# Cross-attention on one core: k and z transposed by the DMA instead of TensorE, and first scores behind two query tiles

## The chip, the cores and the metric

The kernel runs on one core of a Trainium2 chip. The metric is the device time of one execution in microseconds (us), the time of the slowest core, here the only one.

## The reference

Eight batches of `x` and `ctx`, 256 rows of 1024 features each; 32 heads of 32 features.

```python
mu, var = mean(x), var(x)
z = (x - mu) * rsqrt(var + LN_EPS) * ln_gamma + ln_beta
Q = split_heads(z @ Wq.T); K = split_heads(ctx); V = split_heads(ctx)
scores = einsum('bhsd,bhtd->bhst', Q, K) * 32 ** -0.5
scores = where(mask, scores, -inf)
attn = einsum('bhst,bhtd->bhsd', softmax(scores), V)
out = x + attn @ Wout.T
```

## The kernel before, in words

**Numbers.** Every float32 operand of a product is kept as two float16 values, hi and lo (the rest after hi), and a product is three float16 passes (hi·hi, hi·lo, lo·hi). For the scores the three passes lie on top of each other in the contraction: `q_stack` holds for each head 32 rows of hi, 32 of lo, 32 of hi, then a row of ones; `k_stack` holds hi, hi, lo, then the mask row and three constant rows that carry the log-sum-exp in the second pass. So one matmul contracts over 97 rows (first pass) or 100 (second).

**Stages.** A prologue transposes Wq and Wout (TensorE writes the transpose of a 128x128 block to PSUM, ScalarE takes hi, VectorE lo), normalises and transposes x of batch 0, and makes its q. Then come eight iterations, one for each batch b. In **phase S**, 16 steps n = 0..15 (four heads and 128 query rows each), TensorE makes scores (`scores_s`, L499), VectorE their maximum (L826), ScalarE exponentials with row sums (L653). In **phase T**, eight groups g with two steps each, TensorE makes the scores transposed and already normalised (`scores_t`, L525), ScalarE takes the exponential (L670), TensorE multiplies by v (`probs_times_v`, L537) and the result is split into `aT` (L676, L861). Between these steps TensorE does output-projection matmuls of batch b-1 (L478, 7 in each S step, `O_AT`) and q matmuls of batch b+1 (L453, in the last two S steps and in T). Score tiles are double buffered, so step n waits for step n-2.

**The operands of the next batch.** In S steps 0 to 3 TensorE also transposes z of batch b+1 (`z_transposes`, L415, from `x_nat` that VectorE has normalised at L817), and in steps 6 to 9 k (`k_transposes`, L428). VectorE scales them out of PSUM into `t_f32` (L769 with gamma and beta, L777), GpSimd (POOL) splits them into hi and lo (L326 to L338). Then SP, whose queue is strictly in the order of the program, issues twelve copies and a mask copy for each half of `k_stack` (`fill_k_stack`, L168, L172), twelve for each half of `q_stack` (`fill_q_stack`, L189), and the rows of the log-sum-exp (`fill_l_rows`, L203), for which the first `scores_t` of each half waits. `add_residual` (L868) on VectorE stands in S steps 6, 8, 11 and 14; the seventh output matmul of step 6 begins a new PSUM tile and waits for the one of step 6.

**Order.** Everything is written out by hand: each engine has its own program and waits on semaphores. The first scores of batch 0 stand behind all four q tiles and half of Wout; the other eight Wout blocks (`WO_STEPS`) lie in iteration 0.

## Time and profile before

| | |
|---|---|
| median of 3 runs | 629.6 us (628.39 to 630.53) |
| the profiled execution: its own time | 630.62 us |
| its span | 628.8 us |
| mean granted TensorE clock | 0.975 |
| prologue, to the first scores | 60 us |
| iteration 0 | 68 us |
| iterations 1 to 6 | 70.3 us each |
| iteration 7 with the last projection | 77.8 us |

The span runs from the first to the last instruction of the profiled execution; its own time is 1.8 us more. The iterations are read off by the first scores of each batch, which repeat every 70.3 us. Busy time says how long an engine had an instruction in it, idle time with its releaser says what it waited for; the chain of work that ended last gives, piece by piece, what set the pace.

### The profile page before, as it was taken

The numbers are of one execution on the slowest core, as the hardware profiler recorded it, in microseconds if no ns is written. First come the engines' busy times: TensorE is split into PE (matmuls) and PEld (weight loads), VectorE is DVE, ScalarE is ACT, GpSimd is POOL, SyncE is SP. The second block draws the span as 40 slices with busy tenths as digits, with TensorE's granted clock in tenths as the row PEclk, the third lists the DMA queues.
The fourth block names the chain that finished last, engine by engine and source line by source line (L and its number), as shares of the span: only waits on it lengthen the run. The fifth ranks groups of instructions, "written<-read, shape, count | busy, mean of one in ns | idle before, by whom it ended". The sixth has DMA issues, their size and how long they took to land.

```text
span 628.8 us, 12852 instructions
## 1 busy us (share of the span) xinstructions
PE 589.5 (94%) x4769; PEld 396.2 (63%) x4769; DVE 385.0 (61%) x841; ACT 430.8 (69%) x1321; POOL 112.8 (18%) x131
## 2 busy tenths in 40 slices
PE   4878879999999999999999999999999999998897
PEld 4667657655776567655776567755776567644443
DVE  5575977478654885388654886288645882278211
ACT  3342978778766886678766886678666885699740
POOL 2320440035000530044000520044001520000000
PEclk9889689999999999999999999999999999999899
DMA  9774321443344252343344152333344132321202
GB/s 282 267 223 128 114 73 55 122 126 99 106 117 130 60 163 56 107 117 105 100 125 130 52 170 57 99 119 109 96 124 134 63 89 57 98 51 67 71 1 101
DMA packets 37344, 68.62 MB, mean 109 GB/s; under 512 B 9009, under 2 KB 11041, under 8 KB 37282
## 3 DMA queue, kind: packets, MB, share of 16 engines
q1 hardware_dynamic: 36994, 67.60, 35.9%
q8 instruction: 38, 0.62, 0.4%
q10 hardware_dynamic: 288, 0.20, 0.1%
q14 instruction: 24, 0.20, 0.1%
HBM read 33.56 MB, written 8.39 MB: 67 GB/s over the span
## 4 chain that ended last, share of the span: by engine, by line
PE 71%; DVE 14%; ACT 8%; issue 3%; DMA 2%; ACTq 1%; SPq 1%; DVEq 0%
PE mm L453 24%; PE mm L478 17%; PE pv L537 10%; PE score L525 9%; PE score L499 6%; DVE nmax L826 6%; ACT score L653 6%; PE pv L415 2%; PE pv L428 2%; DMA ctx_sb<-in_ctx 1%; ACT probs L670 1%; DVE o_buf L868 1%; PE pv L382 1%; DVE wqT L748 1%; DVE t_f L777 1%
## 5 line engine op out<-in xcount | busy, mean ns | idle before, releaser
L653 ACT ACTIVATE score<-score,nmax 128x256 f32<-128x256 f32 x512 | 230.1, 465 | 47.7 <-DVE nmax L826 47.6
L453 PE MATMUL mm<-zT,wqT 128*128 128x256 f16 x1536 | 186.6, 276 | 0.0
L826 DVE TENSOR_REDUCE nmax<-score 128x2 f32<-128x512 f32 x256 | 163.8, 684 | 37.0 <-PE score L499 36.9
L478 PE MATMUL mm<-woT,aT 128*128 128x512 f16 x768 | 183.6, 379 | 1.5 <-DVE o_buf L868 1.5
L670 ACT ACTIVATE probs<-score 128x1024 f32<-128x1024 f32 x128 | 123.9, 1022 | 73.4 <-PE score L525 73.1
L453 PEld LDWEIGHTS mm<-zT,wqT 128*128 128x128 f16 x1536 | 151.5, 99 | 23.0 <-issue 2.9
L478 PEld LDWEIGHTS mm<-woT,aT 128*128 128x128 f16 x768 | 74.7, 97 | 73.2 <-DVE o_buf L868 4.4
L653 ACT ACTIVATION_READ_ACCUMULATOR score<-score,nmax 128x1 f32 x512 | 114.7, 224 | 0.0
L861 DVE TENSOR_TENSOR aT<-pv,aT 128x256 f16<-128x256 f32 x64 | 26.9, 423 | 114.7 <-ACT aT L676 113.9
L499 PE MATMUL score<-k_stack,q_stack 97*128 97x256 f16 x512 | 79.6, 279 | 10.5 <-ACT score L653 9.4
L499 PEld LDWEIGHTS score<-k_stack,q_stack 97*128 97x128 f16 x512 | 47.9, 99 | 46.4 <-ACT score L653 22.9
L326 POOL CAST zT<-t_f 128x512 f16<-128x512 f32 x28 | 17.1, 609 | 322.0 <-DVE t_f L769 322.0
L525 PE MATMUL score<-q_stack,k_stack 100*128 100x256 f16 x512 | 68.3, 276 | 2.0 <-ACT probs L670 1.1
L537 PE MATMUL pv<-probs,ctx_sb 128*32 128x256 f32 x1024 | 69.4, 389 | 0.9 <-DVE aT L861 0.6
L525 PEld LDWEIGHTS score<-q_stack,k_stack 100*128 100x128 f16 x512 | 45.7, 98 | 29.2 <-issue 18.1
L537 PEld LDWEIGHTS pv<-probs,ctx_sb 128*32 128x32 f32 x1024 | 27.5, 110 | 25.9 <-ACT probs L670 8.0
L645 ACT ACTIVATE qT<-mm 128x512 f16<-128x512 f32 x32 | 19.5, 608 | 23.0 <-PE mm L453 23.0
L782 DVE SCALAR_TENSOR_TENSOR qT<-mm,qT 128x512 f16<-128x512 f32 x32 | 22.0, 689 | 20.5 <-ACT qT L645 20.0
L328 POOL TENSOR_TENSOR zT<-t_f,zT 128x512 f16<-128x512 f32 x28 | 32.3, 1155 | 2.2
L338 POOL TENSOR_TENSOR kT<-t_f,kT 128x512 f16<-128x512 f32 x28 | 32.3, 1155 | 2.2
L868 DVE SCALAR_TENSOR_TENSOR o_buf<-mm,res 128x512 f32<-128x512 f32 x32 | 21.7, 679 | 17.3 <-PE mm L478 17.3
L676 ACT ACTIVATE aT<-pv 128x256 f16<-128x256 f32 x64 | 24.8, 390 | 9.0 <-PE pv L537 9.0
(62 smaller groups left out, 352.2 us busy)
## 6 DMA issues: line engine op xcount, KB each, us to landing
k_stack<-kT SPq DMA_DIRECT2D x192, 64.0 KB, 2.0
q_stack<-qT SPq DMA_DIRECT2D x180, 64.0 KB, 2.0
x_nat<-in_x SPq DMA_DIRECT2D x8, 1024.0 KB, 5.4
ctx_sb<-in_ctx SPq DMA_DIRECT2D x8, 1024.0 KB, 6.3
res<-in_x SPq DMA_DIRECT2D x32, 256.0 KB, 2.9
out<-o_buf SPq DMA_DIRECT2D x32, 256.0 KB, 2.0
probs<-in_L_xattn_Wq SPq DMA_DIRECT2D x8, 512.0 KB, 7.8
probs<-in_L_xattn_Wout SPq DMA_DIRECT2D x8, 512.0 KB, 4.5
```

The lines of the kernel that those rows point to most:

```text
L328: pool.tensor_tensor(zT[:, 1, at], t_f32[:, f % 2], zT[:, 0, at], ALU.subtract).then_inc(split_done, 1)
L338: pool.tensor_tensor(kT[:, 1, at], t_f32[:, f % 2], kT[:, 0, at], ALU.subtract).then_inc(split_done, 1)
L453: last = pe.matmul(mm[i % 2][:, m2 * S:(m2 + 1) * S], wqT[:, wp, k, m * P:(m + 1) * P], zT[:, zp, k, :], start=(v2 == 0), stop=(v2 == KT * ...
L478: last = pe.matmul(mm[i % 2][:], aT[:, ap, k, st * P:(st + 1) * P], woT[:, wp, k, nh * 512:(nh + 1) * 512], start=(v == 0), stop=(v == O_M ...
L499: last = pe.matmul(score[n % 2][:, j, :], q_stack[0:S_ROWS, h, j, gl, st * P:(st + 1) * P], k_stack[0:S_ROWS, pb, h, j, gl, :], start=True ...
L525: last = pe.matmul(score[n % 2][:, j, :], k_stack[0:T_ROWS, pb, h, j, gl, tt * P:(tt + 1) * P], q_stack[0:T_ROWS, h, j, gl, :], start=True ...
L537: last = pe.matmul(pv[g % 2][DH * j:DH * (j + 1), 0, :], ctx_sb[:, pb, tt, g * P + DH * j:g * P + DH * (j + 1)], probs[:, g % 2, tt, j, :] ...
L653: last = act.activation(score[n % 2][:, j, :], score[n % 2][:, j, :], ACT.Exp, bias=nmax[:, st, h, j, gl:gl + 1], accum_out=sums[:, st, h, ...
L670: act.activation(probs[:, g % 2, tt], score[n % 2][:], ACT.Exp).then_inc(exp_done, 1)
L826: dve.tensor_reduce(nmax[:, st, h, at, gl], score[n % 2][:, at, :], AX.X, ALU.max, negate=True).then_inc(max_done, 1)
L861: dve.tensor_tensor(aT[:, 1, g, :], pv[g % 2][:, 0, :], aT[:, 0, g, :], ALU.subtract).then_inc(a_lo, 1)
L868: dve.scalar_tensor_tensor(out=o_buf[:, i % 2, :], in0=mm[i % 2][:], scalar=1.0 / W_SCALE, in1=res[:, i % 2, :], op0=ALU.mult, op1=ALU.add ...
```

## The change

k and z are no longer transposed by TensorE. z is normalised with gamma and beta in its natural layout by VectorE in two passes (`centre`, `normalise`), k stays as it came. GpSimd splits both in natural layout: for k it writes, for 16 heads and 128 rows at a time (one of four pieces c), 32 columns of hi, 32 of hi, 32 of lo and 32 extra ones (mask, constants) side by side. Then SP issues DMA transposes: four for z (256 KB each) and four for k (512 KB each) of a batch. k's transposed block is the stack itself, so its 24 row copies and two mask copies fall away. The natural pieces lie in `probs`, which is free in phase S (for batch 1 in `aT`, `res`, `o_buf`; for batch 0 in the other half of `k_stack`). GpSimd's pieces 2 and 3 of k wait until pieces 0 and 1 have been transposed; ScalarE's first exponentials of phase T wait for the transposes to be done with `probs`. In the prologue the first scores stand behind two q tiles; the other two, the last two Wq blocks, centring of batch 1 and all sixteen Wout blocks lie in iteration 0. The kernel's factors of 0.5 on k and 2 on q are gone.

```diff
+            def turn_z(a):
+                for st in range(ST):
+                    sp.wait_ge(z_lo, (a - 1) * ST + st + 1)
+                    if a == 1 and st == 0:
+                        sp.wait_ge(q_ready, FILLS)
+                    for part in range(2):
+                        sp.dma_start_transpose(zT[:, part, :, st * P:(st + 1) * P], z_nat(a)[:, st, part]).then_inc(z_in, DMA)
+
+            def turn_k(a, pa, c):
+                sp.wait_ge(k_done, 2 * (4 * a + c + 1))
+                if a == 1 and c == 0:
+                    for h in range(2):
+                        sp.wait_ge(k_in[h], 2 * DMA)
+                sp.dma_start_transpose(k_turned(pa, c), k_nat(a, c).rearrange("p n d -> p (n d)")).then_inc(k_in[c // 2], DMA)
...
-                if not first and not last:
-                    sp.wait_ge(pv_ready, b * G)
-                    load_c(b + 1, 1 - pb)
                 if not first:
+                    if not last:
+                        sp.wait_ge(pv_ready, b * G)
+                        load_c(b + 1, 1 - pb)
                     sp.wait_ge(q_lo, b * FILLS + 4)
                     fill_q_stack(1)
+                    if not last:
+                        turn_z(b + 1)
                     store_out(b - 1, 0)
                     load_res(b - 1, 2)
+                    if more:
+                        load_x(b + 2)
+                    if not last:
+                        turn_k(b + 1, 1 - pb, 0)
+                        turn_k(b + 1, 1 - pb, 1)
                     store_out(b - 1, 1)
                     load_res(b - 1, 3)
-                if not last:
-                    fill_k_stack(b + 1, 1 - pb, 0)
-                if more:
-                    sp.wait_ge(fill_ready, z_fill(b + 1, 3) + 1)
-                    load_x(b + 2)
-                if not first:
+                    if not last:
+                        turn_k(b + 1, 1 - pb, 2)
+                        turn_k(b + 1, 1 - pb, 3)
                     store_out(b - 1, 2)
                 fill_l_rows(b, 0)
                 fill_l_rows(b, 1)
...
-                             rows[0:1, r, :].unsqueeze(1).to_broadcast([1, 2 * H, S])).then_inc(row_in, DMA)
-            sp.wait_ge(mask_ok, 1)
-            sp.dma_start(mask_add, mask_st).then_inc(mask_in, DMA)
-            for n in range(4, KT):
-                load_w(n)
+            sp.wait_ge(ones_done, 2)
+            sp.dma_start(q_stack[96:97].rearrange("o h j g s -> o (h j g) s"), one_f16.unsqueeze(1).to_broadcast([1, H, S])).then_inc(row_in, DMA)
+            load_w(4)
+            load_w(5)
+            turn_k(0, 0, 0)
             sp.wait_ge(z0_ready, FILLS)
...
+            turn_k(0, 0, 1)
+            load_w(6)
+            turn_k(0, 0, 2)
+            load_w(7)
+            turn_k(0, 0, 3)
             load_c(1, 1)
...
+            sp.wait_ge(q_hi, 1)
+            for j in range(J):
+                sp.dma_start(q_stack[0:DH, 0, j, 0:2], qT[DH * j:DH * (j + 1), 0, 0:2, :]).then_inc(q0_in, DMA)
             load_w(KT)
+            fill_q0_tile_1()
             load_w(KT + 1)
-            fill_q0_tile(0, (0, 1))
...
-            fill_q0_tile(1, range(J))
-            fill_k_stack(0, 0, 1)
+            sp.wait_ge(q_lo, FILLS)
+            fill_q_stack(1)
             load_w(KT + 4)
             load_w(KT + 5)
-            sp.wait_ge(q_lo, FILLS)
-            fill_q_stack(1)
+            turn_z(1)
+            load_x(2)
             load_w(KT + 6)
             load_w(KT + 7)
+            for c in range(4):
+                turn_k(1, 1, c)
...
+            def z_split(a, st):
+                pool.wait_ge(norm_done, a * ST + st + 1)
+                if a > 1 and st == 0:
+                    pool.wait_ge(pv_ready, (a - 1) * G)
+                pool.tensor_copy(z_nat(a)[:, st, 0], x_nat[:, st]).then_inc(z_hi, 1)
+                pool.wait_ge(z_hi, (a - 1) * ST + st + 1)
+                pool.tensor_tensor(z_nat(a)[:, st, 1], x_nat[:, st], z_nat(a)[:, st, 0], ALU.subtract).then_inc(z_lo, 1)
...
+                pool.tensor_copy(to[:, :, 0:2 * DH].rearrange("p n (r d) -> p n r d", r=2), of.unsqueeze(2).to_broadcast([P, HEADS, 2, DH])).then_inc(k_hi, 1)
+                pool.tensor_copy(to[:, :, 3 * DH:3 * DH + K_EXTRA], k_extra[:, a, tt].unsqueeze(1).to_broadcast([P, HEADS, K_EXTRA])).then_inc(k_done, 1)
+                pool.wait_ge(k_hi, 4 * a + c + 1)
+                pool.tensor_tensor(to[:, :, 2 * DH:3 * DH], of, to[:, :, 0:DH], ALU.subtract).then_inc(k_done, 1)
+
+            for c in range(4):
+                k_split(0, 0, c)
+
+            pool.wait_ge(q_hi, 1)
+            for j in range(J):
+                pool.dma_start(q_stack[2 * DH:3 * DH, 0, j, 0:2], qT[DH * j:DH * (j + 1), 0, 0:2, :]).then_inc(q0_pool_in, DMA)
...
+                pe.wait_ge(ones_done, 2)
+                pe.wait_ge(gb_in, 2 * DMA)
+                for i, bank in enumerate((mm[0], mm[1], pv[0], pv[1])):
+                    row = (gamma_row, beta_row)[i // 2][:, i % 2 * 512:(i % 2 + 1) * 512]
+                    to = bank[:] if i < 2 else bank[:].rearrange("p c s -> p (c s)")
+                    pe.matmul(to, one_f32, row, start=True, stop=True).then_inc(gb_ready, 1)
...
                     elif u == 0:
-                        pe.wait_ge(split_done, z_fill(a, 3) + 1)
+                        pe.wait_ge(z_in, a * 2 * ST * DMA)
...
                 else:
-                    pe.wait_ge(wq_lo, W_FILLS - 2 + 2 * n)
+                    pe.wait_ge(wq_lo, 8 + 2 * n)
...
-            Q_AT_STEP_FIRST = [0] * 6 + [9 * n for n in range(11)]
-            Q_AT_FIRST = [104 + 11 * g for g in range(G)] + [187, Q_ALL]
+
+            Q0_AT = [2 * Q_MM + 24 * n for n in range(5)]
+            Q_AT_STEP_FIRST = [0] * 12 + [0, 16, 32, 48, 64]
+            Q_AT_FIRST = [96 + 12 * g for g in range(G)] + [186, Q_ALL]
...
-                    if not last:
-                        if n in Z_STEPS:
-                            z_transposes(b + 1, Z_STEPS.index(n), b)
-                        if n in K_STEPS:
-                            k_transposes(b + 1, 1 - pb, K_STEPS.index(n), b)
+                    if first and n < 4:
+                        q_matmuls(0, Q0_AT[n], Q0_AT[n + 1], None)
+                    if first and n == 0:
...
             for i in range(FILLS):
                 z0_transposes(i)
             for f in range(4, 8):
                 wq_transposes(f)
             q_matmuls(0, 0, Q_MM, None)
-            for f in range(8, 12):
+            for f in range(8, 10):
                 wq_transposes(f)
-            for i in (2, 3):
-                k0_transposes(i)
             q_matmuls(0, Q_MM, 2 * Q_MM, None)
-            for f in range(12, W_FILLS):
+            for f in range(10, WQ_EARLY):
                 wq_transposes(f)
-            for f in range(WO_FIRST // 2):
-                wo_transposes(f)
-            q_matmuls(0, 2 * Q_MM, 3 * Q_MM, None)
-            for f in range(WO_FIRST // 2, WO_FIRST):
-                wo_transposes(f)
-            q_matmuls(0, 3 * Q_MM, 4 * Q_MM, None)
-            pe.wait_ge(row_in, (1 + L_ROWS) * DMA)
             iteration(0, 0, True, False)
...
+                if first and n == 0:
+                    act.wait_ge(wo_ready, W_FILLS)
+                elif n == 0 and not last:
+                    act.wait_ge(k_in[1], 2 * (b + 2) * DMA)
+                elif n == 2 and not first and not last:
+                    act.wait_ge(z_in, (b + 1) * 2 * ST * DMA)
                 act.activation(probs[:, g % 2, tt], score[n % 2][:], ACT.Exp).then_inc(exp_done, 1)
...
+
+            def centre(a, st):
+                dve.wait_ge(rstd_step, (a + 1) * RSTD_STEPS)
+                if known(a, 0):
+                    dve.wait_ge(gb_done, 4)
+                dve.scalar_tensor_tensor(out=x_nat[:, st], in0=x_nat[:, st], scalar=mean_var[:, st, 0:1], in1=gamma_b[:],
+                                         op0=ALU.subtract, op1=ALU.mult).then_inc(centre_done, 1)
+
             def normalise(a, st):
-                dve.wait_ge(rstd_step, (a + 1) * RSTD_STEPS)
-                dve.tensor_scalar(x_nat[:, st], x_nat[:, st], mean_var[:, st, 0:1], rstd[:, st:st + 1],
-                                  ALU.subtract, ALU.mult).then_inc(norm_done, 1)
+                dve.wait_ge(centre_done, a * ST + st + 1)
+                dve.scalar_tensor_tensor(out=x_nat[:, st], in0=x_nat[:, st], scalar=rstd[:, st:st + 1], in1=beta_b[:],
+                                         op0=ALU.mult, op1=ALU.add).then_inc(norm_done, 1)
...
                 for n in range(STEPS):
                     max_step(b, n)
-                    if not last:
-                        if n - 1 in Z_STEPS:
-                            z_scale(b + 1, Z_STEPS.index(n - 1))
-                        if n - 1 in K_STEPS:
-                            k_scale(b + 1, K_STEPS.index(n - 1))
+                    if first and 1 <= n < 5:
+                        if n == 1:
+                            for f in range(WQ_EARLY, W_FILLS):
+                                wq_split(f)
+                        if n < 3:
+                            centre(1, n - 1)
+                        else:
+                            normalise(1, n - 3)
+                    if first and n in (2, 4):
+                        q_split(0, 1 + n // 2)
                     if first and n - 1 in WO_STEPS:
-                        wo_split(WO_FIRST + WO_STEPS.index(n - 1))
-                    if first and n == Q_STEP_FIRST:
-                        q_split(b + 1, 0)
+                        for f in WO_STEPS[n - 1]:
+                            wo_split(f)
```

TensorE, phase S of batch 1, steps 0 to 3 and 6 of before (`x_nat` is x of the next batch, `ctx_sb` its k):

```order
L499 MATMUL score<-k_stack,q_stack 128x256 x4
L415 MATMUL pv<-ident,x_nat 128x128 x4
L478 MATMUL mm<-woT,aT 128x512 x7
L499 MATMUL score<-k_stack,q_stack 128x256 x4
L415 MATMUL pv<-ident,x_nat 128x128 x4
L478 MATMUL mm<-woT,aT 128x512 x7
...
L499 MATMUL score<-k_stack,q_stack 128x256 x4
L428 MATMUL pv<-ident,ctx_sb 128x128 x4
L478 MATMUL mm<-woT,aT 128x512 x7
```

The same steps of the change:

```order
L501 MATMUL score<-k_stack,q_stack 128x256 x4
L478 MATMUL mm<-woT,aT 128x512 x7
L501 MATMUL score<-k_stack,q_stack 128x256 x4
L478 MATMUL mm<-woT,aT 128x512 x7
L501 MATMUL score<-k_stack,q_stack 128x256 x4
```

Eight groups of four transposes have left the row; scores and output matmuls follow each other directly.

SP, from the last `q_stack` copies of a batch to the log-sum-exp rows, before:

```order
L189 DMA q_stack<-qT 32x1024 x12
L214 DMA out<-o_buf 128x512
L209 DMA res<-in_x 128x512
L214 DMA out<-o_buf 128x512
L209 DMA res<-in_x 128x512
L168 DMA k_stack<-kT 32x1024 x12
L172 DMA k_stack<-k_stack 1x16x256
L152 DMA x_nat<-in_x 128x2x1024
L214 DMA out<-o_buf 128x512
L203 DMA q_stack<-l_rows 1x16x256 x6
```

and of the change:

```order
L208 DMA q_stack<-qT 32x1024 x12
L195 DMA_TRANSPOSE zT<-probs 128x8x128 x4
L235 DMA out<-o_buf 128x512
L230 DMA res<-in_x 128x512
L174 DMA x_nat<-in_x 128x2x1024
L202 DMA_TRANSPOSE k_stack<-probs 128x16x128 x2
L235 DMA out<-o_buf 128x512
L230 DMA res<-in_x 128x512
L202 DMA_TRANSPOSE k_stack<-probs 128x16x128 x2
L235 DMA out<-o_buf 128x512
L221 DMA q_stack<-l_rows 1x16x256 x6
```

All eight transposes now stand ahead of the log-sum-exp rows in SP's queue; before, one half of the k copies did, the other came behind them.

TensorE, from the first q tile to step 4 of the first batch, in the change (before, 4 blocks of 48 L453 and eight Wout blocks stood ahead of the first scores):

```order
L453 MATMUL mm<-zT,wqT 128x256 x48
L402 MATMUL score<-ident,probs 128x128 x8
L453 MATMUL mm<-zT,wqT 128x256 x48
L402 MATMUL pv<-ident,probs 128x128 x16
L501 MATMUL score<-k_stack,q_stack 128x256 x4
L453 MATMUL mm<-zT,wqT 128x256 x24
L402 MATMUL pv<-ident,probs 128x128 x8
L501 MATMUL score<-k_stack,q_stack 128x256 x4
L453 MATMUL mm<-zT,wqT 128x256 x24
```

Two q tiles are cut into four pieces of 24 matmuls and stand behind scores 0 to 3.

## Rows read from the trace of the kernel before

**Rows 1.** The page, busy time and share of the span of each engine.

```profile
PE 589.5 (94%) x4769; PEld 396.2 (63%) x4769; DVE 385.0 (61%) x841; ACT 430.8 (69%) x1321; POOL 112.8 (18%) x131
```

**Rows 2.** Busy time by stretch: length, engines, granted clock, DMA share, GB/s.

```profile
61.00:129.00 68.00, 60.35 (x516) 44.44 (x514) 48.37 (x106) 54.32 (x168) 14.11 (x16) 0.87 0.31 87
340.10:410.40 70.30, 69.17 (x582) 46.77 (x580) 45.75 (x102) 51.25 (x160) 14.12 (x16) 1.00 0.36 107
551.00:628.80 77.80, 69.08 (x446) 32.70 (x444) 33.05 (x66) 47.56 (x156) 0.00 (x0) 0.97 0.18 59
```

**Rows 3.** The chain of waits in iteration 4: start us, us, what.

```profile
346.98 0.44 PE pv L415 x4
347.42 1.51 PE mm L478 x7
348.94 0.44 PE score L499 x4
...
353.92 0.68 DVE nmax L826
354.61 0.61 DVE o_buf L868
355.26 0.39 PE mm L478
...
364.58 0.60 DVE t_f L777
...
374.04 5.02 PE mm L453 x46
```

**Rows 4.** Groups by line: xcount, busy us, mean ns of one, idle before.

```profile
L415 PE MATMUL pv<-ident,x_nat 128*128 128x128 f32 x112 | 18.2, 287 | 0.2
L861 DVE TENSOR_TENSOR aT<-pv,aT 128x256 f16<-128x256 f32 x64 | 26.9, 423 | 114.7 <-ACT aT L676 113.9
L855 DVE TENSOR_TENSOR l_rest<-l_rest,l_rows 16x256 f32<-16x256 f32 x16 | 6.6, 413 | 0.6
L336 POOL CAST kT<-t_f 128x512 f16<-128x512 f32 x28 | 17.1, 610 | 42.5 <-DVE t_f L777 42.5
L338 POOL TENSOR_TENSOR kT<-t_f,kT 128x512 f16<-128x512 f32 x28 | 32.3, 1155 | 2.2
```

**Rows 5.** Timeline of SP's queue in iteration 4: start us, us issuing, what.

```profile
339.65 8.01 SPq L189 DMA_DIRECT2D q_stack<-qT  x12
372.53 13.14 SPq L203 DMA_DIRECT2D q_stack<-l_rows  x6
```

**Rows 6.** DMA issues: xcount, KB each, median us from issue to landing.

```profile
probs<-in_L_xattn_Wq SPq DMA_DIRECT2D x8, 512.0 KB, 7.8
q_stack<-l_rows SPq DMA_DIRECT2D x48, 8.0 KB, 1.8
```

**Rows 7.** Busy time by stretch, the ten us in which the DMA moved most.

```profile
30.00:40.00 10.00, 8.90 (x80) 7.87 (x78) 5.77 (x10) 6.43 (x13) 3.48 (x4) 1.00 1.02 295
```

**Rows 8.** Timeline of VectorE and TensorE in the prologue: start us, us, what.

```profile
11.87 1.54 DVE L817 TENSOR_SCALAR x_nat<-x_nat,mean_var,rstd 128x1024 f32<-128x1024 f32 x2
...
21.80 6.40 PE L453 MATMUL mm<-zT,wqT 128*128 128x256 f16 x48
...
59.98 0.60 PE L499 MATMUL score<-k_stack,q_stack 97*128 97x256 f16 x4
```

**Rows 9.** The chain of waits in iteration 0: Wq and Wout splits, exponentials.

```profile
34.20 2.48 DVE wqT L748 x4
...
99.53 0.49 ACT woT L638
100.02 1.82 ACT score L653 x8
...
103.19 1.84 ACT probs L670 x2
...
128.33 0.55 PE score L499 x4
```

445 lines of the change are left out of this document (194 added, 251 removed).

## The prediction

> **What bounds the kernel now.** I read the page first: TensorE is busy 94% of the span, ScalarE 69%, VectorE 61%, GpSimd 18% [rows 1]. A share is an average, so next came the busy time by stretch: iterations 1 to 6 are alike, 70.3 us long with 69.2 us of TensorE, iteration 0 takes 68.0 us at a granted clock of 0.87, and the last stretch is the loosest [rows 2]. The chain of waits then says what a TensorE instruction is worth. In phase S it runs along TensorE: four transposes 0.44 us, seven output matmuls 1.51, four scores 0.44 [rows 3]. A step with transposes lasts 2.39 us, one without 1.95. Phase T is TensorE alone, and nothing is removed there. So what leaves TensorE in phase S is worth its time, down to the next limit. That limit is near: ScalarE needs 1.82 us for a step's eight instructions [rows 9], against 1.95 on TensorE.
>
> **Iterations 1 to 6, what is removed.** Eight steps lose 0.44 us each, 3.5 us. One is no gain: in step 6 the seventh output matmul waits for VectorE's maximum and residual, until 355.26 [rows 3]; without transposes TensorE arrives 0.44 us earlier and waits 0.44 longer, since VectorE starts only once the scores are there. Near the end of phase S the chain is VectorE's, and k's last scaling stands in it with 0.60 us [rows 3]; it goes, but TensorE's own pace of 1.95 a step comes next, so I count 0.4. Together 7 x 0.44 + 0.4 = 3.5 us an iteration, 6 x 3.5 = **21 us**. The bounds are 2.6 (ScalarE's waits eat two steps) and 3.9 (step 6 gains too). Iteration 7 has nothing to lose.
>
> **What is added there, on VectorE.** Two normalising instructions of 0.8 us (1.54 for a pair [rows 8]) become four with two SBUF inputs. The nearest row is L855, 413 ns for 256 elements [rows 4], about 0.15 us plus an element a ns; so some 1.2 us for 1024, and 4.8 - 1.5 = 3.3 us more. They stand in phase T, groups 3 to 6, where VectorE sat idle for 114.7 us over 64 splits, 14 us a batch [rows 4]. Cost zero; without that cover 20 us in six iterations.
>
> **On GpSimd.** Per batch: z twice 1024 elements cast and subtracted, 2 x (2 x 0.61 + 2 x 1.16) = 7.1 us by the 512-element rows L336 and L338 [rows 4]; k four pieces of 1024 cast, 512 copied, 512 subtracted, 1.2 + 0.6 + 1.2 = 3.0 us each. That is 19 us in 67, hidden, but its order matters: z is ready 3.5 and 7 us into phase S, k's pieces 0 and 1 at 10 and 13, pieces 2 and 3 only after the first two have been turned.
>
> **On SP: the term that decides.** Let t be the time that one k piece (512 KB) holds the queue; a z piece is half. No row shows a DMA transpose. From below: the DMA moved 295 GB/s at its fullest [rows 7], 512 KB in 1.8 us. From above: eight 64 KB copies at SP's 8.01 / 12 = 0.67 us [rows 5], 5.3 us. The queue after the start of phase S: twelve q copies until 8.3 us; z until 8.3 + 2t; the output store not before 14 (residual of step 6), some loads 1.2; k 0 and 1, 2t; landing about 2 (the 8 KB copies land in 1.8 [rows 6]); GpSimd 3.0 to 6.0; k 2 and 3; then the log-sum-exp rows, three issues of 0.6 and 1.8 to land. `scores_t` wants them when the q matmuls of 5.02 us [rows 3] are done, at 31.4 + 5.0 = 36.4 us. With t = 1.8 all is turned at 28.7 and the rows land at 32.5: no wait. With t of 3 or more SP never idles, and they land at 18.6 + 6t, which is on time up to t = 3.0. I take t = 2, near the lower end: a transpose is one issue and moves the bytes of one 512 KB load, not of eight row copies. **Cost zero.**
> The Trainium skill (Advanced Engine Details and Errata, X-Bar Transpose (TRN2)) says that such transposes run at 350 to 400 GB/s, which would make t about 1.4, an estimate; no run here shows it yet. It changes nothing in the sum. Against the change speaks the skill's VectorE: DVE Perf Modes, The three transpose paths: 1309 ns by DMA for a 128x128 block where TensorE takes 390. If these did not overlap, a k piece of 16 blocks would take 21 us and the kernel over 900; an estimate by that page, which the sum does not use.
>
> **Prologue and iteration 0.** Before: q starts at 21.8 us, first scores at 60.0, first exponentials of phase T at 103.2, next batch at 128.3 [rows 8, 9]. Now: the mask, gamma and beta stand ahead of VectorE's chain (about 2 us) and normalising takes 3.3 us more; the splits after it are the same. I put q's start at 26 to 27. Two q tiles of 6.4 and 5.4, six groups of Wq transposes, with VectorE's second statistics between, bring the first scores to **44 us**, 16 earlier. But their work moves into phase S. Steps 0 to 4 hold on VectorE five maxima (6.5 us), two Wq splits (1.2, by 2.48 for four [rows 9]), four normalising passes (4.8), two q splits (1.4), 14 us, plus waits for 24 q matmuls at a time: 17.6. Then ScalarE sets the pace: eleven steps of 1.82 + 0.49 and four more Wout splits, 27.4, plus 2 for the log-sum-exp. First exponentials at 91 instead of 103.2, **12 us** won. Phase T costs 0.7 more (12 q matmuls a group for 11) and batch 1's k pieces 2 and 3 are turned late, 1 to 2 us. Net **10 us**, from 5 to 16.
>
> **Sum.** The profiled execution took 630.6 us, 1.0 over the median of 629.6. 630.6 - 21 - 10 = 599.6, against the median **599 us**.
>
> **Rivals.**
> A, *slower queue*: t = 3.4, between the two ends. The rows land at 39.0 instead of 36.4, and seven phases T start 2.6 us late: 599 + 18 = **617 us**. For it: SP needs 0.67 us even for 64 KB. Against: a 512 KB load lands in 7.8 us at the crowded start [rows 6], with others ahead of it. Chance 0.14.
> B, *SP's queue becomes the bound* (the other sign): one mechanism, the eight transposes ahead of the log-sum-exp rows. At t = 5.3 they land at 50.4, 14 us late, seven times over: 599 + 98 = **697 us**. It turns the gain of 31 into a loss from 4.4 us of wait per batch, t = 3.8. TensorE's clock would then dip in each wait, as in iteration 0. The skill's 1309 ns lies far beyond. Chance 0.10.
> C, *VectorE and GpSimd in each other's way in the prologue*: k's four pieces run on GpSimd from about 12 to 24 us, the four normalising passes on VectorE fall into that time. No row shows a long two-input VectorE instruction beside GpSimd. If each waits for a GpSimd instruction of 1.2 us and Wq's splits shift with them, q starts 5 us later, and waits of step 0 to 4 take 5 more: **609 us**. The skill's SBUF - State Buffer, section SBUF: two separate sides, says that a VectorE operation with two SBUF inputs and a GpSimd operation exclude each other; the trace of before has no such pair to test it. Chance 0.12.
> D, *the gain is there but smaller*, ScalarE's 1.82 against 1.95 leaving less than I count: 2.6 an iteration, 604; inside my own range.
>
> **How the numbers follow.** My forecast (t up to 3, prologue as worked) has 0.64, and its own range is 590 to 608: the ends are 16 us of prologue with 3.9 an iteration, and 5 us with 2.6. C 0.12, A 0.14, B 0.10. The range of 590 to 620 takes in the forecast, C and A, and leaves out B and the tails. About 0.3% (1.9 us) is what a measurement of this kernel can tell from no change; all cases but B lie well below, so faster 0.87, same 0.02, slower 0.11.
>
> **What would show it.** Right: no transposes of L415 and L428, steps of 1.95 us in phase S, the iteration at 66.8 us; transposes in SP's timeline at about 2 us each; first scores at 44 us, batch 1 at 118. Wrong: TensorE waiting at `scores_t` for the log-sum-exp rows, ScalarE at its first exponential for k, POOL's k piece 2 late, the granted clock below 1.00 in iterations 1 to 6; or normalising passes longer than 1.2 us while GpSimd works.

## The result and the profile after

The changed kernel takes **656.7 us** (median of 4 runs, 653.9 to 661.8) against 629.7 (628.4 to 630.5) for the kernel before in the same session: ratio 1.0445, 95% interval 1.0392 to 1.0497. It is slower by 27 us; the forecast was 599, range 590 to 620. One of the four runs of experiment 2 (649.0 us) lay over 1.5% above the fastest of its kernel and is left out of the ratio there. The profiled execution took 655.7 us with a span of 653.9 at a mean granted clock of 0.945.

| us in the profiled execution | before | forecast | after |
|---|---|---|---|
| first q tile starts | 21.8 | 26 to 27 | 36.0 |
| first scores of batch 0 | 60.0 | 44 | 56.2 |
| batch 1 starts | 128.3 | 118.3 | 157.4 |
| iterations 1 to 6 together | 421.7 | 400.7 | 418.6 |
| iteration 7 and the last projection | 78.9 | 78.9 | 78.0 |

The lines of the table run from the first scores of one batch to those of the next. So read, batch 7 of the kernel before starts at 549.9 us, and its last stretch is 78.9 us long, where the table of the kernel before and the stretch 551.0 to 628.8 in [rows 2] have 77.8; an iteration is 70.28 us. The forecast lay 56.1 us below the profiled execution, and two lines hold it: 39.1 us up to batch 1, and 17.9 in iterations 1 to 6, less 0.9 at the end. The page of the kernel after, engines and DMA:

```profile
PE 578.7 (89%) x4537; PEld 380.6 (58%) x4537; DVE 387.6 (59%) x772; ACT 430.8 (66%) x1321; POOL 133.6 (20%) x134
DMA packets 123422, 79.86 MB, mean 122 GB/s; under 512 B 101762, under 2 KB 103202, under 8 KB 123364
```

TensorE lost 232 instructions and 10.8 us of busy time against [rows 1], yet its share fell from 94 to 89%: it waits more.

**A steady iteration.** In iteration 3, SP's queue from the start of batch 3's phase S (start, us issuing, what):

```profile
297.58 0.39 SPq L177 DMA_DIRECT2D ctx_sb<-in_ctx  x1
298.01 7.48 SPq L208 DMA_DIRECT2D q_stack<-qT  x12
305.53 6.21 SPq L195 DMA_TRANSPOSE zT<-probs  x4
...
312.90 0.45 SPq L174 DMA_DIRECT2D x_nat<-in_x  x1
313.72 7.87 SPq L202 DMA_TRANSPOSE k_stack<-probs  x2
...
326.95 4.67 SPq L202 DMA_TRANSPOSE k_stack<-probs  x2
331.66 0.97 SPq L235 DMA_DIRECT2D out<-o_buf  x1
332.68 1.97 SPq L221 DMA_DIRECT2D q_stack<-l_rows  x3
```

The chain of waits through the same place, in order of time:

```profile
319.56 4.36 DMA k_stack<-probs
...
323.98 1.04 POOL probs L358
...
334.06 2.84 DMA q_stack<-l_rows
...
336.95 1.05 PE score L525 x8
```

and TensorE there (idle time and its releaser in brackets):

```profile
329.69 0.61 PE L501 MATMUL score<-k_stack,q_stack 97*128 97x256 f16 x4 [2.13 <-ACT score L655]
330.13 5.19 PE L453 MATMUL mm<-zT,wqT 128*128 128x256 f16 x46
336.95 1.05 PE L525 MATMUL score<-q_stack,k_stack 100*128 100x256 f16 x8 [1.63 <-DMA q_stack<-l_rows]
```

Read from the top: the twelve q copies keep time, z's turns take 6.2 us, the first two k turns 7.9, they land 4.4 us after the issue, and only then may GpSimd write pieces 2 and 3 over the buffer. Their turns and a store follow, then the log-sum-exp rows, which land at 336.9, 39.3 us into the iteration; the q matmuls were done 37.7 into it. The busy time by stretch shows how full the DMA was meanwhile, in the first row those of pieces 0 and 1, in the second the whole iteration:

```profile
313.70:321.60 7.90, 7.90 (x46) 4.36 (x45) 6.31 (x14) 7.86 (x36) 0.00 (x0) 1.00 0.99 253
297.58:367.57 69.99, 65.54 (x550) 43.37 (x549) 44.49 (x92) 51.08 (x160) 17.23 (x16) 1.00 0.56 129
```

The DMA engines are full (0.99) while k is turned, behind 1 MB of x that was issued just before.

Iteration 3 is not typical in one thing: TensorE waits for the log-sum-exp rows in three of the six iterations only, 0.5, 1.6 and 0.5 us in iterations 2, 3 and 5. In all six it waits at step 15 for ScalarE, 2.0 to 2.8 us, and in three of them it then runs its q matmuls at a lower clock. Iteration 1, the slowest with 70.5 us, in three views: VectorE's log-sum-exp operations, TensorE's step 15, and the stretch behind it.

```profile
184.62 0.75 DVE L853 CAST l_rows<-l_rest 16x256 f16<-16x256 f32 x1
185.40 1.26 DVE L855 TENSOR_TENSOR l_rest<-l_rest,l_rows 16x256 f32<-16x256 f32 x1
186.69 1.01 DVE L857 TENSOR_SCALAR l_rows<-l_rest 16x256 f16<-16x256 f32 x1
```

```profile
190.32 0.61 PE L501 MATMUL score<-k_stack,q_stack 97*128 97x256 f16 x4 [2.82 <-ACT score L655]
190.77 6.85 PE L453 MATMUL mm<-zT,wqT 128*128 128x256 f16 x46
```

```profile
190.30:197.50 7.20, 7.18 (x51) 5.81 (x52) 2.85 (x8) 4.66 (x19) 0.00 (x0) 0.76 0.50 113
```

The three operations take 0.28, 0.41 and 0.28 us in the kernel before. Here GpSimd is at k's pieces 2 and 3 from 183.6 us on, beside them; the next maximum on VectorE, ScalarE's exponentials and step 15 come later by as much. The 46 matmuls take 6.85 us at a granted clock of 0.76 and 5.19 at full clock (iteration 3 above).

**Prologue.** VectorE's chain for the first rstd, and TensorE's first instructions, in two views:

```profile
13.20 0.23 DVE L939 TENSOR_SCALAR k_extra<-score 128x16 f16<-128x16 f32 x1 [5.75 <-PE score L387]
...
15.25 1.09 DVE L791 TENSOR_SCALAR newton<-var_eps 128x2 int32<-128x2 int32 x1
16.38 0.94 DVE L793 TENSOR_SCALAR rstd<-newton 128x2 int32<-128x2 int32 x1
17.36 0.51 DVE L797 TENSOR_TENSOR newton<-rstd 128x2 f32<-128x2 f32 x1
...
24.32 0.16 DVE L797 TENSOR_TENSOR newton<-rstd 128x2 f32<-128x2 f32 x1
```

```profile
5.97 3.75 PE L383 MATMUL mm<-res,l_rows 1*128 1x512 f32 x4 [5.97 <-DMA o_buf<-in_L_xattn_ln_beta]
9.52 3.62 PE L383 MATMUL pv<-o_buf,l_rows 1*128 1x512 f32 x4
12.93 0.23 PE L387 MATMUL score<-ident,l_rest 16*128 16x16 f32 x1
...
35.97 5.40 PE L453 MATMUL mm<-zT,wqT 128*128 128x256 f16 x48 [0.64 <-DVE wqT L747]
```

Two faults come together, and the first brings on the second. The mask's small transpose stands behind the row products of gamma and beta, 7.4 us, and VectorE stands behind the mask in its own program. So its chain falls into the time in which GpSimd splits k (13.60 to 24.27), and the same two-element instructions take up to 1.09 us instead of 0.16, and fall back the moment it stops. In iteration 0, steps 12 to 15 read like this on TensorE:

```profile
109.88 3.44 PE L453 MATMUL mm<-zT,wqT 128*128 128x256 f16 x16
113.15 0.60 PE L501 MATMUL score<-k_stack,q_stack 97*128 97x256 f16 x4
115.83 1.68 PE L416 MATMUL pv<-ident,probs 128*128 128x128 f32 x8 [2.07 <-DVE woT L755]
117.30 3.15 PE L453 MATMUL mm<-zT,wqT 128*128 128x256 f16 x16
```

A step takes 7.1 us (113.15 to 120.29), not 2.3: scores, 2.1 us of wait for the split of the last Wout tile, transposes, then the q matmuls, one after the other. The mean granted clock from 102 to 125 us is 0.72, so TensorE ran part of this at 1.2 and part at 2.4 GHz.

### The profile page after: what moved, and what is told of

It is laid out like the page before. It is cut to its first block, busy times and chain, and to the rows that moved or that the text cites. A ratio compares the mean times of both kernels' runs of the same rounds, so it can differ in the third digit from the quotient of the medians.

```text
span 653.9 us, 12077 instructions
## 1 busy us (share of the span) xinstructions
PE 578.7 (89%) x4537; PEld 380.6 (58%) x4537; DVE 387.6 (59%) x772; ACT 430.8 (66%) x1321; POOL 133.6 (20%) x134
## 2 busy tenths in 40 slices
DMA packets 123422, 79.86 MB, mean 122 GB/s; under 512 B 101762, under 2 KB 103202, under 8 KB 123364
## 4 chain that ended last, share of the span: by engine, by line
PE 62%; SPq 11%; DVE 10%; ACT 7%; DMA 5%; issue 3%; POOL 3%; ACTq 1%; DVEq 0%
PE mm L453 23%; PE mm L478 13%; PE pv L537 9%; PE score L525 9%; ACT score L655 5%; PE score L501 5%; SPq L202 3%; SPq L208 3%; DVE nmax L824 3%; DMA k_stack<-probs 2%; SPq L195 2%; DMA q_stack<-l_rows 1%; POOL probs L361 1%; PE pv L416 1%; POOL probs L358 1%
## 5 line engine op out<-in xcount | busy, mean ns | idle before, releaser
L453 PE MATMUL mm<-zT,wqT 128*128 128x256 f16 x1536 | 194.0, 284 | 0.6 <-DVE wqT L747 0.6
L478 PE MATMUL mm<-woT,aT 128*128 128x512 f16 x768 | 183.6, 379 | 4.1 <-DVE o_buf L868 4.1
L453 PEld LDWEIGHTS mm<-zT,wqT 128*128 128x128 f16 x1536 | 156.0, 102 | 27.4 <-issue 3.7
L501 PE MATMUL score<-k_stack,q_stack 97*128 97x256 f16 x512 | 81.0, 282 | 24.1 <-ACT score L655 17.8
L525 PEld LDWEIGHTS score<-q_stack,k_stack 100*128 100x128 f16 x512 | 45.4, 98 | 31.8 <-issue 18.5
L341 POOL CAST probs<-x_nat 128x1024 f16<-128x1024 f32 x12 | 12.4, 1036 | 235.5 <-PE pv L537 235.5
L358 POOL CAST probs<-ctx_sb 128x1024 f16<-128x1024 f32 x24 | 25.4, 1060 | 84.1 <-DMA k_stack<-probs 83.1
L868 DVE SCALAR_TENSOR_TENSOR o_buf<-mm,res 128x512 f32<-128x512 f32 x32 | 21.8, 680 | 17.3 <-PE mm L478 17.3
L361 POOL TENSOR_TENSOR probs<-ctx_sb,probs 128x512 f16<-128x512 f32 x24 | 28.3, 1178 | 0.0
```

The lines of the kernel that those rows point to most:

```text
L358: pool.tensor_copy(to[:, :, 0:2 * DH].rearrange("p n (r d) -> p n r d", r=2), of.unsqueeze(2).to_broadcast([P, HEADS, 2, DH])).then_inc(k_ ...
L361: pool.tensor_tensor(to[:, :, 2 * DH:3 * DH], of, to[:, :, 0:DH], ALU.subtract).then_inc(k_done, 1)
L453: last = pe.matmul(mm[i % 2][:, m2 * S:(m2 + 1) * S], wqT[:, wp, k, m * P:(m + 1) * P], zT[:, zp, k, :], start=(v2 == 0), stop=(v2 == KT * ...
L478: last = pe.matmul(mm[i % 2][:], aT[:, ap, k, st * P:(st + 1) * P], woT[:, wp, k, nh * 512:(nh + 1) * 512], start=(v == 0), stop=(v == O_M ...
L501: last = pe.matmul(score[n % 2][:, j, :], q_stack[0:S_ROWS, h, j, gl, st * P:(st + 1) * P], k_stack[0:S_ROWS, pb, h, gl, j, :], start=True ...
L525: last = pe.matmul(score[n % 2][:, j, :], k_stack[0:T_ROWS, pb, h, gl, j, tt * P:(tt + 1) * P], q_stack[0:T_ROWS, h, j, gl, :], start=True ...
```

## The experiments

Each was made from the changed kernel. Two theories stood at first. **Order:** the added work fits, but stands in the wrong place of a queue (SP's, TensorE's, or GpSimd against VectorE). **Worth:** what left phase S had not been worth 3.5 us, or the transposes are too dear whatever the order.

**1. The mask first.**

```diff
-            gb_rows()
             pe.wait_ge(ident_ok, 1)
             mask_transpose()
+            gb_rows()
```

> Edit: TensorE transposes the mask before it multiplies gamma and beta out to 128 rows, not behind it. Theory P (prologue): in the change VectorE's second statistics of batch 0 stand behind the mask (13.2 us), and that puts the rstd chain (14.9 to 25.1, 3.3 us of work) into the time in which GpSimd splits k (13.6 to 24.3). With the mask first, the chain runs at 8 to 12 us beside an idle GpSimd, in 3.3 us; gamma and beta (four products, some 7.2 us) then bound the centring, at about 14; q starts at 24 to 27 us instead of 36.0, and the kernel takes about 646 us instead of 656.7. Rival: the first scores (56.2 us) are bound by k's transposes in SP's queue or by the second rstd chain and not by q; then q starts earlier, but the kernel gains under 3 us. A third possibility, VectorE's two-input centring beside GpSimd: L810 and L815 then take 2 to 3 us each instead of 1.24, and half of the gain is lost.

Measured: 647.2 us, ratio to before 1.0241 (1.0185 to 1.0298); q starts at 26.7, first scores at 46.75, batch 1 at 147.7, which is 9.3, 9.4 and 9.7 us earlier; the median time is 9.5 us less (four runs, 641.2 to 650.1). In the profiled execution, 650.1 us, iterations 1 to 6 took 4.6 us more than in the changed kernel, two of them 72.6 and 73.2. So the prologue gives back what was expected, and that the median does so to the tenth is in part luck. The rstd chain runs from 8.9 to 11.8, in 3 us, since GpSimd still waits for its context load until 12.2. The mutual hold has moved to the four normalising passes. VectorE, then GpSimd:

```profile
14.25 3.72 DVE L810 SCALAR_TENSOR_TENSOR x_nat<-x_nat,mean_var,gamma_b 128x1024 f32<-128x1024 f32 x2 [2.41 <-ACT beta_b L622]
17.90 3.72 DVE L815 SCALAR_TENSOR_TENSOR x_nat<-x_nat,rstd,beta_b 128x1024 f32<-128x1024 f32 x2
```

```profile
14.86 2.04 POOL L358 CAST k_stack<-ctx_sb 128x1024 f16<-128x1024 f32 x1
```

1.86 us a pass, and GpSimd's cast takes 2.04 us where it takes 1.04 alone: both lose.

**2. In a step of iteration 0, q matmuls ahead of Wout's transposes.**

```diff
-                    if first and n in WO_STEPS:
-                        for f in WO_STEPS[n]:
-                            wo_transposes(f)
...
                         q_matmuls(b + 1, at[n], at[n + 1], c)
+                    if first and n in WO_STEPS:
+                        for f in WO_STEPS[n]:
+                            wo_transposes(f)
```

> Edit: in steps 12 to 15 of iteration 0 TensorE does its 16 q matmuls before the two Wout blocks, not behind them. Theory W: those four steps take 7.2 us each because they are one serial chain, scores, maximum, split of the last step's Wout block, this step's two blocks, 16 q matmuls (2.9 to 3.4 us, at half clock), next scores. With q first the matmuls run beside maximum and split, a step takes 3.5 to 4.5 us, and the kernel takes 645 us instead of 656.7. Rival: TensorE's own work at the low clock (0.5 to 0.7 granted) sets them; then a step takes 5 us or more and the gain is 8 us or less. Rival: batch 1's k, turned late through SP's queue (to 113.4 us), takes over; gain under 4 us.

Measured: 644.5 us, ratio 1.0164 (1.0115 to 1.0213), 12 us less, 8.2 of which lie before batch 1, which starts at 149.2. TensorE:

```profile
104.56 0.60 PE L501 MATMUL score<-k_stack,q_stack 97*128 97x256 f16 x4
105.00 1.91 PE L453 MATMUL mm<-zT,wqT 128*128 128x256 f16 x16
107.23 1.23 PE L416 MATMUL pv<-ident,probs 128*128 128x128 f32 x8 [0.32 <-DVE woT L755]
108.29 0.60 PE L501 MATMUL score<-k_stack,q_stack 97*128 97x256 f16 x4
...
119.51 1.89 PE L525 MATMUL score<-q_stack,k_stack 100*128 100x256 f16 x8 [3.83 <-DMA q_stack<-l_rows]
```

Steps fall from 7.1 to 3.73 us: the q matmuls now fill the time in which the tile is split. And a new wait appears behind them, 3.8 us for the log-sum-exp rows, whose place in SP's queue is behind batch 1's k turns.

**3. The x load behind the log-sum-exp rows.**

```diff
-                    if more:
-                        load_x(b + 2)
...
                 fill_l_rows(b, 0)
+                if more and not first:
+                    load_x(b + 2)
```

> Edit: the 1 MB load of x two batches ahead is issued behind the first log-sum-exp rows instead of just ahead of k's first transpose (batch 1 on). Theory Q1: SP's queue sets iterations 1 to 6, and its longest single piece, 5.8 us for the first k transpose against 2.0 for the later ones, is that transpose held back behind the load. Then it falls to 2 to 3 us, an iteration takes 67 instead of 69.8, and the kernel 639 us instead of 656.7. Rival Q2: it is held back by the z transposes and q copies ahead of it, whose descriptors are many; then it stays at 4.5 us or more, and the kernel within 5 us of 656.7.

Measured: 645.6 us, ratio 1.0227 (1.0196 to 1.0257). That is 11 us less where 18 were expected: the first pair of k turns falls from 7.9 to 9.3 us to 5.1 to 6.4, but iterations lie between 67.7 and 70.5. TensorE now waits for the log-sum-exp rows in none of the six, so the bytes of x ahead of the turns were what made them late. What is left stands in another place: at step 15 it still waits 1.6 to 2.8 us for ScalarE, and in the two iterations of 70.3 and 70.5 the clock falls behind that wait (0.76 and 0.77 over the q matmuls).

**4. A buffer of its own for k's pieces 2 and 3**, from batch 2 on, so that GpSimd need not wait for the first turns.

```diff
+        k_more = sb("k_more", [P, 2, HALF * J, P], F16)
...
+            elif c >= 2:
+                return k_more[:, c % 2]
```

> Edit: k's pieces 2 and 3 are split into a buffer of their own (8 KB a partition) from batch 2 on, so GpSimd doesn't wait for the transposes of pieces 0 and 1. Theory G: the chain of iterations 1 to 6 goes q copies, z, k 0 and 1, their landing, 5.7 us of GpSimd, k 3, log-sum-exp rows; without the wait it loses landing and GpSimd, some 6 to 8 us, which is more than the 3 us that phase S can shrink by, so an iteration takes 67 us instead of 69.8 (the last five of the six), the kernel 643, and VectorE's L857 falls from 531 to 281 ns since GpSimd is no longer at work beside it. Rival: the queue itself is full, k 2 and 3 are held up as long as k 0 was, and the gain is under 5 us.

Measured: 638.5 us, ratio 1.012 (1.009 to 1.015), 18 us less; iterations of 66.8 to 68.9. GpSimd's 14.6 us of wait is gone, and so is its work beside VectorE's log-sum-exp operations: the three of 16x256 from SBUF take 413, 281 and 280 ns, as before, instead of 628, 531 and 425. TensorE's wait at step 15 is 0.8 us in all six iterations, and the clock stays at full speed. Still, in four of the six the log-sum-exp rows come late, by 0.3 to 1.9 us, behind the turns of pieces 2 and 3. Of the 18 us, 13.0 lie in iterations 1 to 6. Another 5.1 lie before batch 1, where this edit changes nothing; the granted clock between 102 and 125 us was 0.85 here and 0.72 in the changed kernel. So the start of batch 1 can differ by some 5 us between profiled executions without a cause in the edit, and a difference of that size in it can't be put down to an edit.

**5. GpSimd held back in the prologue** until x of batch 0 is normalised.

```diff
+                    pool.wait_ge(norm_done, ST)
```

> The changed kernel with one wait more: GpSimd starts on batch 0's k pieces only when VectorE has normalised x (everything else as changed). Theory L (VectorE and GpSimd hold each other up on SBUF operands): the rstd chain, which took 10.2 us beside GpSimd's k split and 3.3 us in the kernel before, takes about 3.5 us again and the four normalising operations about 1.24 us each, so q starts at about 29 us instead of 36.0 and batch 1 at about 151 instead of 157.4: about 650 us, 6 less than the changed kernel. Rival M (it is only the late gamma/beta row products that make the prologue late): the chain still takes about 10 us with GpSimd idle and the time stays at 656. If k's turned pieces now come too late for the first scores, the gain is smaller than 6 us and TensorE's first score waits for k_stack instead of for q_stack.

Measured: VectorE and TensorE do as theory L says, in two views:

```profile
16.04 0.16 DVE L804 TENSOR_TENSOR rstd<-rstd,newton 128x2 f32<-128x2 f32 x1
...
17.82 2.48 DVE L811 SCALAR_TENSOR_TENSOR x_nat<-x_nat,mean_var,gamma_b 128x1024 f32<-128x1024 f32 x2
```

```profile
28.68 5.40 PE L454 MATMUL mm<-zT,wqT 128*128 128x256 f16 x48 [1.28 <-DVE wqT L748]
```

The chain takes 3.0 us instead of 10.2, the passes 1.24 each, q starts 7.3 us earlier, and rival M falls. But first scores come 3.6 and batch 1 only 5.0 us earlier: TensorE stands idle 5.4 us before the first scores, whose q copies SP issues at 45.4, behind k's turns and a 1 MB load. And the total is 655.0 us (652.3 to 656.2), ratio 1.039 (1.0361 to 1.0419): 1.7 us less where 6 were expected. In the profile 4.2 us are given back in iterations 1 to 6, two of which last 71.8 and 71.9 us. Those are the two in which the first pair of k turns took 10.7 and 11.1 us, and TensorE waited 3.1 and 3.2 us for the log-sum-exp rows; in the three others with an x load ahead of it the pair took 7.9 to 9.4, in the last 4.7, and they last 69.7 to 69.9. Why the same turns behind the same loads take longer in these two I can't say; it stays open.

**6. The log-sum-exp rows ahead of k's last two turns**, with the buffer of experiment 4, now for batch 1 too.

```diff
-                    if not last:
-                        turn_k(b + 1, 1 - pb, 2)
-                        turn_k(b + 1, 1 - pb, 3)
                     store_out(b - 1, 2)
                 fill_l_rows(b, 0)
+                if not first and not last:
+                    turn_k(b + 1, 1 - pb, 2)
+                    turn_k(b + 1, 1 - pb, 3)
```

> The kernel with a second buffer for k's pieces (0, 1 apart from 2, 3), and from batch 1 on the log-sum-exp rows leave SP's queue ahead of the turns of pieces 2 and 3. Theory Q (the steady iteration was set by SP's queue: z's turns, k's first turns, then k's last turns, all ahead of the log-sum-exp rows): iterations take 66.8 us or a little less instead of 69.7 in the changed kernel and 67.7 with the buffer alone, and the time is about 632 us (638.5 with the buffer alone). Rival N (the TensorE work that left phase S was worth less than 3.5 us, whatever the queue does): iterations stay at 67.5 to 68 and the time at 637 to 638.

ScalarE's first exponentials of phase T now wait for pieces 0 and 1 alone, since 2 and 3 no longer lie in `probs`. Measured: 636.2 us, ratio 1.010 (1.0085 to 1.0115). Each of the iterations 1 to 6 is now 66.84 or 66.85 us. Busy time by stretch of iteration 3 (batch 3's phase S on), and SP's queue in it:

```profile
289.68:356.52 66.84, 65.37 (x550) 43.45 (x549) 43.13 (x92) 51.12 (x160) 16.89 (x16) 1.00 0.60 135
```

```profile
305.74 7.70 SPq L205 DMA_TRANSPOSE k_stack<-probs  x2
...
317.84 1.82 SPq L224 DMA_DIRECT2D q_stack<-l_rows  x3
319.70 5.79 SPq L205 DMA_TRANSPOSE k_stack<-k_more  x2
```

The turns are not faster (7.7 and 5.8 us), and no one waits for them. So rival N falls: what left phase S was worth its 3.5 us. The total is 4 us above the expectation. In the profiles batch 1 starts at 155.9 here and at 152.3 in experiment 4: between 102 and 125 us TensorE was granted a clock of 0.72 here and of 0.85 there, with the same serial steps in both. The expectation had built on experiment 4's luck.

**7 and 8. The repairs together,** without and with GpSimd held back. To the edits of 1, 2, 4 and 6 come: the x load behind the last k turns, batch 1's k turns ahead of the last two Wout loads, and in iteration 0 `q_split` ahead of the normalising pass of its step.

```diff
+                    if first and n in (2, 4):
+                        q_split(0, 1 + n // 2)
...
-                    if first and n in (2, 4):
-                        q_split(0, 1 + n // 2)
```

> All the separate repairs together: mask ahead of gamma and beta, q's rows split before the centring in iteration 0, the second k buffer, log-sum-exp rows ahead of the last k turns, the next x load behind these turns, and batch 1's first k turns ahead of the last two loads of Wout; Wout's own block work behind a step's scores. If the gains are of separate places they add: prologue 9.5 (mask) and about 12 (q first), steady iterations (69.7 - 66.5) x 6 = 19 us, some 5 more for the turns ahead of Wout's loads: 656.7 - 45 = about 611 us. If they share one bound (SP's queue in iteration 0), the sum falls short: about 620 us.

> The same, with GpSimd held back until VectorE has normalised x of batch 0. Theory L: the normalising operations fall from 1.86 to 1.24 us each, q starts 2 us earlier than in the run without the wait; the time is 2 us less, unless k's turned block then comes after q's second tile (first score waiting for k_stack), which makes it equal or up to 3 us more.

Measured: 616.7 (615.2 to 617.5) and 616.6 us (615.7 to 618.1), ratios 0.9793 (0.9774 to 0.9812) and 0.9789 (0.9768 to 0.981). Both are 2.1% faster than the kernel before, and lie between the two expectations of 7, 611 for separate gains and 620 for a shared bound. Iterations 1 to 6 take 66.84 each; batch 1 starts at 135.0 and 134.5. In 8 q starts at 25.0 against 27.1 in 7, 2 us as expected, yet the first scores come 1.4 us later (48.7 against 47.3), with TensorE idle 4.6 us ahead of them, batch 1 gains only 0.5, and the time is the same. Limits stand behind q's start; those of iteration 0 can be seen in 8. Between 70 and 90 us, by stretch:

```profile
70.00:90.00 20.00, 16.05 (x71) 10.87 (x72) 15.61 (x31) 17.51 (x69) 12.22 (x13) 0.51 0.96 223
```

TensorE runs at a granted clock of 0.51, half speed (1.2 GHz), and the DMA engines are 96% busy. The last Wout block lands at 98.7, and TensorE waits for it:

```profile
98.72 1.09 PE L420 MATMUL pv<-ident,probs 128*128 128x128 f32 x8 [2.22 <-DMA probs<-in_L_xattn_Wout]
```

**9 and 10. Three commands of SP in iteration 0 moved; then the context load of batch 1 behind the first q copies.**

```diff
             turn_z(1)
-            load_x(2)
-            for c in range(4):
-                turn_k(1, 1, c)
+            turn_k(1, 1, 0)
+            turn_k(1, 1, 1)
             load_w(KT + 6)
             load_w(KT + 7)
+            turn_k(1, 1, 2)
+            turn_k(1, 1, 3)
+            load_x(2)
```

> The repaired kernel (616.6 us) with three SyncE commands of iteration 0 in another order: Wout's last two loads between k's turns 1 and 2 of batch 1, batch 2's x load behind the last turn. In the repaired kernel the last Wout block was issued at 94.6 us and landed at 98.7, with TensorE idle 2.2 us for it and VectorE 3.3 us. Theory D (iteration 0 is held by 1 MB and 512 KB transfers in one queue, the DMA engines being 96% busy between 70 and 90 us): the last Wout block lands at about 91 us, the wait goes, batch 1 starts at about 131 instead of 134.6, time about 613. Rival C (steps 12 to 15 are a serial chain of score, maximum and Wout's split at their own durations): 616 still.

> The same, and batch 1's context load (1 MB) behind the copies of the first q tiles instead of ahead of them. In the repaired kernel TensorE waited from 44.0 to 48.7 us for these copies, issued from 42.15 on behind three turns and this load. Theory D: first scores 1 to 2 us earlier, time 1 to 2 us less than the run beside it; otherwise the same.

Measured: 612.1 us (611.3 to 613.1), ratio 0.972 (0.9696 to 0.9744), and **609.6 us** (609.2 to 610.4), ratio 0.9679 (0.9661 to 0.9698). In 9 the wait for Wout is gone and batch 1 starts at 131.7; in 10 first scores stand at 45.4 instead of 48.3 and batch 1 starts at 129.4. Theory D holds, rival C falls. Ten's start of batch 1, six iterations of 66.84 us and 77.4 for the last add to its span of 607.8.

## Why the prediction failed, step by step

**Iterations 1 to 6, what is removed: right.** The forecast said 66.8 us an iteration; with the order mended it is 66.84 (experiments 6 to 10), a gain of 3.4 on 70.28 where 3.5 was worked out. That step 6 gains nothing is seen by itself: TensorE's wait there grows from 0.25 to 0.68 us. The q matmuls end 36.4 us into the iteration in experiment 6, as forecast. How the rest divides among the steps was not measured.

**"Cost zero" for SP and "hidden" for GpSimd: this step failed,** and it cost 17.5 of the 21 us. Counted over all six iterations of the changed kernel against experiment 6:

| us more than in experiment 6, iteration | 1 | 2 | 3 | 4 | 5 | 6 | sum |
|---|---|---|---|---|---|---|---|
| TensorE's wait for ScalarE at step 15 | 2.0 | 2.0 | 1.3 | 1.9 | 1.2 | 1.2 | 9.7 |
| its matmuls behind that wait, at a lower clock | 1.7 | 0 | 0 | 1.4 | 0 | 1.7 | 4.7 |
| its wait for the log-sum-exp rows | 0 | 0.5 | 1.6 | 0 | 0.5 | 0 | 2.5 |
| the iteration | 3.7 | 2.7 | 3.2 | 3.3 | 1.8 | 2.9 | 17.5 |

The first and largest term has no place in the forecast. GpSimd's 19 us in 67 were called hidden, with the remark that their order matters, but nothing was worked out of what VectorE does beside them. k's pieces 2 and 3 came to lie on VectorE's five log-sum-exp operations of phase S (L849 to L857), which took 1.8 us in the kernel before and 2.9 to 3.8 here; the excess is 2.05, 2.04, 1.35, 1.92, 1.17 and 1.22 us in iterations 1 to 6, and the first line of the table, to two places, 2.03, 2.04, 1.34, 1.91, 1.17 and 1.22. Experiment 4 takes GpSimd away from there, and the first two lines go. This is rival C's mechanism in a place where no rival looked for it.

What brought GpSimd there was the sum for SP's queue, and for iteration 3 it can be redone. The time t of a turn was a little short: z's four took 5.4 to 6.4 us where 4 was meant, and k's pairs without a load just ahead 4.6 to 5.0, about 2.4 us each. But with t = 2.4 the forecast's own sum still lands the rows at 34.2 us, ahead of 36.4. Failed was the sum around t. It carried the x load as an issue of 0.4 us among "some loads 1.2", while its 1 MB had to pass the same full DMA engines before k's bytes could: the pair took 7.9 us instead of 4. It began 0.9 us later than meant; a store of 1.0 us stands ahead of the rows and was left out; and the rows took 0.6 us more from first issue to landing. With some tenths between them that makes the 6.3 us by which the rows landed late, at 39.3 us into the iteration where 33 was forecast; and it makes pieces 2 and 3 reach GpSimd at 26.4 us instead of 21.2.

Rival B had the right queue, the eight turns ahead of the log-sum-exp rows, but tied the loss to t = 3.8 or more (its own sum gives 3.7) and to the wait for the rows. That wait came true at t near 2.4 and held only 2.5 of the 17.5 us. The signs named in advance did show: the wait for the rows, GpSimd's piece 2 late, and a granted clock of 0.98 instead of 1.00 in iterations 1, 4 and 6.

**Prologue: failed in two steps.** The text said that mask, gamma and beta stand "about 2 us" ahead of VectorE's chain. VectorE waited 5.75 us: the row products of 1 x 512 in float32, eight records of about 0.9 us, were never priced. Moving the mask ahead of them gave 9.5 us back. The second is rival C's mechanism: the forecast looked for it in the four normalising passes, which in the changed kernel ran after GpSimd had stopped; it struck the sixteen small operations ahead of them, 7.2 us. q's start came out 9.5 us late, of both faults together. GpSimd held back alone gives 7.3 of them back (experiment 5), where rival C had put 5; with 0.12 it was underrated.

The Trainium skill (SBUF - State Buffer, SBUF: two separate sides) says that VectorE and GpSimd exclude each other for a whole instruction when VectorE has two SBUF inputs or runs in a two-port mode. The trace agrees: the operations last 1.09, 0.94 and 0.51 us in turn, beside GpSimd's 1.04, 0.61 and 1.16. The forecast had read the rule for operations with two inputs alone; single-input ones suffer just as much here, L791 with 1.09. And it said that the trace of before has no pair to test the rule. It has one, in seven places: L838, with two SBUF inputs, takes up to 469 ns beside GpSimd's L336, against a median of 172. In the changed kernel GpSimd is elsewhere at that time, and the mean of the same operation falls:

```profile
L838 DVE SCALAR_TENSOR_TENSOR lse<-lse_t,lse_r 128x16 f32<-128x16 f32 x32 | 6.2, 234 | 0.6
L836 DVE SCALAR_TENSOR_TENSOR lse<-lse_t,lse_r 128x16 f32<-128x16 f32 x32 | 4.2, 171 | 0.6
```

**Iteration 0: the largest miss, 27 us from first scores to batch 1** (101.2 against 74). Steps 0 to 4 took 16.7 us, 17.6 in the forecast. Phase T took 26.6, about the forecast's 27. Steps 5 to 11, "ScalarE sets the pace", took 23.9 where about 18 were meant, and from step 12 to the first scores of phase T, meant to take about 11, passed 34.0 (96.8 to 130.8). The forecast had summed each engine's work and taken the largest; the program's order on TensorE makes a chain of it. Scores, the wait for the split of the last Wout tile, transposes and 16 q matmuls follow each other, 7.1 us a step and more, and behind the last one stand 48 q matmuls, 6.5 us with nothing beside them, which were not in the sum. Experiment 2 shows the cause by changing the order alone. In steps 5 to 11 the excess is mostly waits: 3.5 us for the split of a Wout tile, and 4.0 for the twelve q copies. VectorE's last normalising pass, 3.05 us beside GpSimd instead of 1.24, stands ahead of both and can explain 1.8 us of them; the copies themselves hold SP's queue 7.5 us. The granted clock is 0.50 from 86 to 102 us, behind these waits, and four scores take 1.06 us there instead of 0.60.

**The sum by experiments.** Taken from the profiled spans, experiment 10 lies 21.0 us under the kernel before: 20.7 in iterations 1 to 6 and 1.5 at the end, less 1.2 lost up to batch 1. The 21 of the forecast are there; the 10 of prologue and iteration 0 are not. First scores come at 45.4, near the forecast's 44, so iteration 0 holds what is missing: 84.0 us where 74 was forecast. That the queue and the half clock there make most of it is likely from the rows of experiment 8, but no experiment took it further.

## What to carry to other kernels

Price a transfer in a queue by all the bytes that stand ahead of it and by the place of the one small transfer that someone waits for; experiments 4 and 6 gave back the whole gain without making any transfer faster. When work moves from one engine to others, write down for one step the order of instructions on the engine that waits, not only the sum on each. When GpSimd gets new work, look at what VectorE does in those same microseconds, small operations included: five of them, 1.8 us in all, set the pace of the steady iterations here. And read a wait in every iteration before you explain it from one.

## What the runs showed of the hardware

- A DMA transpose of 512 KB from SBUF to SBUF held SP's queue 1.9 us at its shortest, 2.4 as one of a pair and 5 to 8 behind loads of 0.5 and 1 MB; one of 256 KB held it 1.3. The hold is not the transfer: with k's turns alone in flight, the DMA engines were full and moved 216 GB/s, 2.4 us for 512 KB (changed kernel, last two columns):

```profile
110.00:112.00 2.00, 2.00 (x11) 1.39 (x10) 0.00 (x0) 0.60 (x1) 1.35 (x2) 0.50 1.14 216
```

  The Trainium skill (VectorE: DVE Perf Modes, The three transpose paths) gives 1309 ns for one 128x128 block; here sixteen blocks went through in 2.4 us, so they overlap. The 350 to 400 GB/s of the Trainium skill's Advanced Engine Details and Errata, X-Bar Transpose (TRN2), were reached in no such stretch here.
- The transposes come as small packets: 101,762 under 512 B, where the kernel before had 9,009.
- TensorE's granted clock fell behind waits of 2.0 to 2.8 us at step 15 in three of six iterations (0.76 over 190.3 to 197.5 us), and 46 matmuls took 6.85 us instead of 5.19.
- VectorE's operations of 128x2 took 0.51 to 1.09 us beside GpSimd and 0.16 alone; passes of 128x1024 with two SBUF inputs took 1.86 and 1.24, one of them 3.05. GpSimd's cast went from 1.04 to 2.04 us.
